# Head attention: two of the eight high parts of a head written by converting transfers on GpSimd's queue

## The chip, the cores and the metric

The kernel runs on one core of a Trainium2 chip. Its time is the device time of one execution in microseconds (us). Three runs of the kernel before gave 2814.51, 2816.11 and 2816.17 us; the median is 2816.11 us. The trace is that of a separate, profiled execution.

Engines are named as in the profile: PE is TensorE's matmul row and PEld its weight load, DVE is VectorE, ACT is ScalarE, POOL is GpSimd, SP is SyncE, which only issues transfers here.

## The reference

The program is a chain of six sublayers on `x` of shape (4, 1024, 128): a mixture-of-experts layer, an attention with shared query, key and value, the mixture-of-experts layer again, a recurrent layer, a second attention with gates and cumulative sums, and the recurrent layer again. The change touches the first attention alone:

```
b, t, c = x.shape            # 4, 1024, 128; x is the layer-normalised input
y = x.reshape(b, t, nh, hs).transpose(0, 2, 1, 3)        # 16 heads of 8 dimensions
scores = einsum('bhtk,bhsk->bhts', y, y) / sqrt(hs)
attn = softmax(scores)
o = einsum('bhts,bsc->bhtc', attn, x)                    # each head weights all 128 channels
return o.transpose(0, 2, 1, 3).reshape(b, t, nh * c) @ weight
```

There are 4 x 16 = 64 heads in all. For each the scores are 1024 x 1024; a head's output is 1024 x 128.

## The kernel before

Products are kept near float32 by splitting each factor into a high part (a `float32r` copy, rounded by the conversion) and a low part (the float32 value less the high part), and by summing three matmuls: low times high, high times low, high times high. These are lines 88, 89 and 90, in the helper `product`.

`head_attention` runs one block in which every engine has a program written out by hand in program order; semaphores alone tie them. A head is cut into 8 tiles `s` of 128 rows by 1024 columns (`TILES` = 8), and the running number of a tile is `n = 8 h + s`. For a tile

- PE writes the scores (line 797, four matmuls a tile pair stand on four row groups and run side by side), for two tiles at a time,
- ACT takes the exponential from PSUM into `heads_e`, which has four buffers `e[:, s % 4, :]` (line 849), and sums the rows on the way (its second instruction, the accumulator's read, after which `exp_done` is counted),
- the high part `heads_e_hi` is written by ACT for tiles 1, 3, 5, 7 (line 856) and by DVE for tiles 0, 2, 4, 6 (line 907),
- DVE writes the low part `heads_e_lo`, exponential less high part (line 909), tile by tile, and counts `low`,
- PE multiplies the parts with the value's parts into the head's output (`weighted_rows`, lines 88 to 90), six tiles behind the scores (`TRAIL` = 6), so that tiles 0 and 1 of a head follow the scores of tiles 6 and 7 of the same head, and tiles 2 to 7 follow scores of the next head.

Around that, per head: DVE inverts the sums (lines 865 and 868); SP stores them and loads them back spread over all partitions as `heads_scale` (512 KB, line 759); DVE multiplies the head's output by it, two halves, `heads_u` (line 875), ACT and DVE split that (lines 839 and 881), and PE adds the head's product with the output weights (`add_head`). DVE's program has `heads_u` of head h - 1 after tile 5 of head h, and the low parts of `heads_u` after tile 7. PE has `add_head` of head h - 2 after the scores of tiles 6 and 7 and directly ahead of tile 0's products of head h, and that tile's first matmul writes over the output, so it waits until `heads_u` has read it.

The scores' operands come from DRAM by eight transfers of 64 KB a head and side: `heads_right` on SP's queue, `heads_left` on POOL's queue (line 743). POOL does nothing else in this stage. It issues head h + 1's eight loads once head h - 1's last scores are done, a whole head ahead.

Of the kernel before, what the change touches and what calls it, by code (L numbers as in the profile page):

```python
# [73 lines left out]
def f(ap):  # L74

    return ap.bitcast(F32)
# [601 lines left out]
def head_attention(nc, tag, psum, consts, dram, x):  # L678


    with ExitStack() as ctx:
# [12 lines left out]
                  splits=[(dram["head_w"], w_hi[:, :], w_lo[:, :])], copies=[(parts_dram[:, 0, :], 0), (parts_dram[:, 1, :], 1), (parts_dram[:, 2, :], 0)],  # L694
                  copied=copied)

        left = sb(f"{tag}_left", [P, 2, T], F32R)
        right = sb(f"{tag}_right", [P, 2, T], F32R)
        v_hi, v_lo = sb(f"{tag}_v_hi", [P, TOKENS], F32R), sb(f"{tag}_v_lo", [P, TOKENS], F32R)
        e = sb(f"{tag}_e", [P, 4, T])  # L700
        sums = sb(f"{tag}_sums", [P, 2, TILES])
        inverse = sb(f"{tag}_inverse", [P, 2, 32])
        inverse_rows = sb(f"{tag}_inverse_rows", [P, 2, 32])
# [12 lines left out]
        out_done, scaled_ready, u_high, u_low = sem("out"), sem("scaled"), sem("u_high"), sem("u_low")  # L716
        sum_done, added = sem("sum_done"), sem("added")
        HEAD_LOADS = 8
        ACT_HIGH = (1, 3, 5, 7)
        TRAIL = 6  # L720
        COUNT = BATCH * HEADS
        VALUE_BANKS = TOKENS // BANK

        def highs(h, s):

            by_act = sum(i in ACT_HIGH for i in range(s + 1))
            return h * len(ACT_HIGH) + by_act, h * (TILES - len(ACT_HIGH)) + (s + 1 - by_act)

        def turned_value(k):

# [15 lines left out]
        with nc.Block() as block:  # L746
# [18 lines left out]
            @block.gpsimd  # L765
            def _(pool):
                load_head(pool, left, (0, 0), 0, left_loaded)
                load_head(pool, left, (0, 0), 1, left_loaded)
                for h in range(2, COUNT):
                    pool.wait_ge(scores_done, (h - 1) * TILES)  # L770
                    load_head(pool, left, (0, 0), h, left_loaded)

            @block.tensor
            def _(pe):
# [24 lines left out]
                        last.then_inc(scores_done, 1)  # L799

                def weighted_rows(h, s):
                    pe.wait_ge(low, h * TILES + s + 1)
                    at_v = slice(h // HEADS * T + s * P, h // HEADS * T + (s + 1) * P)
                    for half in range(HALVES):
                        at = slice(half * BANK, (half + 1) * BANK)
                        if s == 0:
                            after(pe, scaled_ready, (h - 1) * HALVES + half + 1)
                        last = product(pe, psum[:, OUT + half, :], (v_hi[:, at_v], v_lo[:, at_v]),
                                       (e_hi[:, s, at], e_lo[:, s, at]), first=s == 0, last=s == TILES - 1)
                    last.then_inc(out_done, 1)  # L810
# [22 lines left out]
            @block.scalar  # L833
            def _(act):
                def u_highs(g):
                    after(act, sum_done, g - 1)
                    for half in range(HALVES):
                        act.wait_ge(scaled_ready, g * HALVES + half + 1)
                        act.copy(u_hi[:, g % 2, half, :], u[:, half, :]).then_inc(u_high, 1)

                for k in range(0, 2 * VALUE_BANKS, 2):
                    act.wait_ge(turned, k + 1)
                    act.copy(turned_value(k), psum[:, k % 8, :]).then_inc(v_by_act, 1)
                for n in range(COUNT * TILES):
                    h, s = n // TILES, n % TILES
                    act.wait_ge(scores_done, n + 1)
                    after(act, low, n - 3)
                    wide = psum[:, SCORES + 2 * (s % 2):SCORES + 2 * (s % 2) + 2, :].rearrange("p a b -> p (a b)")
                    act.activation(e[:, s % 4, :], wide, ACT.Exp, scale=HEAD ** -0.5,  # L849
                                   accum_out=sums[:, h % 2, s:s + 1]).then_inc(exp_done, 1)  # L850
                    if s in ACT_HIGH:
                        act.wait_ge(exp_done, n + 1)
                        after(act, out_done, n - (TILES - 1))
                        if n < BATCH:
                            act.wait_ge(copied[n], BATCH_COPIED)
                        act.copy(e_hi[:, s, :], e[:, s % 4, :]).then_inc(act_high, 1)  # L856
                    if s == TILES - 1 and h >= 1:
                        u_highs(h - 1)
                u_highs(COUNT - 1)

            @block.vector
            def _(dve):
                def invert(g):
                    dve.wait_ge(exp_done, (g + 1) * TILES)
                    dve.reciprocal(inverse[:, g % 2, 0:TILES], sums[:, g % 2, :]).then_inc(divided, 1)
# [29 lines left out]
                for n in range(COUNT * TILES):  # L895
                    h, s = n // TILES, n % TILES
                    if s == 0 and h >= 1:
                        invert(h - 1)
                    high_act, high_dve = highs(h, s)
                    if s in ACT_HIGH:  # L900
                        dve.wait_ge(act_high, high_act)
                    else:
                        dve.wait_ge(exp_done, n + 1)
                        after(dve, out_done, n - (TILES - 1))
                        if n < BATCH:
                            dve.wait_ge(copied[n], BATCH_COPIED)
                        dve.tensor_copy(e_hi[:, s, :], e[:, s % 4, :]).then_inc(dve_high, 1)
                        dve.wait_ge(dve_high, high_dve)
                    dve.tensor_tensor(e_lo[:, s, :], e[:, s % 4, :], f(e_hi[:, s, :]), ALU.subtract).then_inc(low, 1)  # L909
                    if s == TRAIL - 1 and h >= 1:  # L910
                        scale_sums(h - 1)
                    if s == TILES - 1 and h >= 1:
# [837 lines left out]
```

## Time and profile before

| | us |
|---|---|
| median of three runs | 2816.11 |
| the profiled execution, its own time | 2814.1 |
| its span, first to last instruction | 2812.3 |
| of it, the head stage | 665 to 1672 |
| PE busy in the head stage | 980.26 of 1007 |
| DVE busy in the head stage | 960.00 of 1007 |
| ACT busy in the head stage | 881.45 of 1007 |

The profiled execution is 2.0 us below the median of the runs and 1.8 us longer than its span. In the head stage TensorE was granted 0.99 of its full clock. PE and DVE both look full there, so the shares don't tell which one holds the other; the order in time within one head does. Times in the tables below are microseconds from the span's start.

### The profile page before, as it was taken

To read this page: it belongs to the slowest core of one execution; us is meant where nothing else is said; L and a number is where in the kernel's file an instruction comes from. 1 tells how busy PE (TensorE), PEld (TensorE's weight loads), DVE (VectorE), ACT (ScalarE), POOL (GpSimd) and SP (SyncE) were. 2 spreads that over 40 slices of the span, in tenths; PEclk is the share of its full clock that TensorE was granted. 3 is DMA by queue.
4 is the path that set the end of the run, shared out by engine and by line. 5 is a ranking of instruction groups with operands and counts; after the bars stand their busy time and mean duration, and the time that the engine had idled before them with its cause. 6 is when DMAs were issued, how large, how long until landed. Compare 5 with 4: busy or idle time off the path is not lost. (4 is left out here: it accounts for less than half of the span.)

```text
span 2812.3 us, 36464 instructions
## 1 busy us (share of the span) xinstructions
PE 2633.2 (94%) x11619; PEld 1977.0 (70%) x11619; DVE 2253.9 (80%) x3349; ACT 1829.7 (65%) x3092; POOL 1232.4 (44%) x1265
## 2 busy tenths in 40 slices
PE   7899999997999999999999997999999989788788
PEld 4688888874666666666666664888888866577566
DVE  5777777777999999999999978777787765578545
ACT  3355555556888888888888863555555555466565
POOL 2466667664232323233333312666666650345200
PEclk9999999998999999999999999999999999789899
DMA  2566666644333333333333323466666610100000
GB/s 63 125 140 137 147 140 131 148 99 150 103 101 103 101 105 99 106 98 107 101 104 100 106 71 75 108 147 143 134 147 146 132 42 1 38 8 8 8 8 30
DMA packets 107391, 271.55 MB, mean 97 GB/s; under 512 B 30784, under 2 KB 35648, under 8 KB 107072
## 3 DMA queue, kind: packets, MB, share of 16 engines
q1 hardware_dynamic: 82192, 235.41, 33.8%
q0 software_dynamic: 24576, 33.62, 4.3%
q8 instruction: 92, 1.51, 0.2%
q14 instruction: 99, 0.81, 0.1%
q10 hardware_dynamic: 432, 0.20, 0.0%
HBM read 258.35 MB, written 10.76 MB: 96 GB/s over the span
## 5 line engine op out<-in xcount | busy, mean ns | idle before, releaser
L628 POOL TENSOR_TENSOR moe_experts_lo<-moe_experts_hidden,moe_experts_hi 128x512 fp32r<-128x512 f32 x512 | 660.9, 1291 | 342.2 <-ACT moe_experts_hi L566 342.1
L909 DVE TENSOR_TENSOR heads_e_lo<-heads_e,heads_e_hi 128x1024 fp32r<-128x1024 f32 x512 | 616.2, 1224 | 25.8
L573 ACT ACTIVATE psum<-psum 128x512 f32<-128x512 f32 x512 | 298.0, 582 | 479.4 <-PE psum L90 479.4
L743 POOL DMA_DIRECT2D heads_left<-heads_parts x512 | 306.7, 612 | 670.2 <-PE psum L797 610.6
L849 ACT ACTIVATE heads_e<-psum 128x1024 f32<-128x1024 f32 x512 | 520.0, 1023 | 107.2 <-PE psum L797 107.2
L600 DVE TENSOR_TENSOR moe_experts_weighted<-moe_spread,psum 128x512 f32<-128x512 f32 x512 | 351.1, 686 | 190.7 <-PE psum L90 186.8
L88 PE MATMUL psum<-heads_e_hi,heads_v_lo 128*128 128x512 f32 x1024 | 429.6, 419 | 18.1 <-DVE heads_u L875 18.1
L88 PE MATMUL psum<-moe_n_hi,moe_w_lo 128*128 128x512 f32 x1024 | 400.8, 391 | 6.0 <-PEq L54 6.0
L89 PE MATMUL psum<-heads_e_lo,heads_v_hi 128*128 128x512 f32 x1024 | 404.1, 395 | 0.0
L90 PE MATMUL psum<-heads_e_hi,heads_v_hi 128*128 128x512 f32 x1024 | 400.9, 392 | 0.0
L89 PE MATMUL psum<-moe_n_lo,moe_w_hi 128*128 128x512 f32 x1024 | 400.1, 391 | 0.0
L90 PE MATMUL psum<-moe_n_hi,moe_w_hi 128*128 128x512 f32 x1024 | 399.8, 390 | 0.0
L605 DVE TENSOR_TENSOR moe_experts_hidden<-moe_experts_weighted,psum 128x512 f32<-128x512 f32 x512 | 352.0, 687 | 34.9 <-POOL moe_experts_lo L628 17.9
L566 ACT CAST moe_experts_hi<-moe_experts_hidden 128x512 fp32r<-128x512 f32 x512 | 313.4, 612 | 1.3 <-DVE moe_experts_hidden L605 1.3
L88 PEld LDWEIGHTS psum<-heads_e_hi,heads_v_lo 128*128 128x128 f32 x1024 | 192.5, 188 | 124.6 <-issue 67.6
L856 ACT CAST heads_e_hi<-heads_e 128x1024 fp32r<-128x1024 f32 x256 | 269.6, 1053 | 8.1
L88 PEld LDWEIGHTS psum<-moe_n_hi,moe_w_lo 128*128 128x128 f32 x1024 | 193.3, 189 | 48.3 <-POOLq L638 7.4
L90 PEld LDWEIGHTS psum<-heads_e_hi,heads_v_hi 128*128 128x128 f32 x1024 | 193.1, 189 | 45.3
L90 PEld LDWEIGHTS psum<-moe_n_hi,moe_w_hi 128*128 128x128 f32 x1024 | 193.3, 189 | 40.3
L89 PEld LDWEIGHTS psum<-moe_n_lo,moe_w_hi 128*128 128x128 f32 x1024 | 193.4, 189 | 40.1
L89 PEld LDWEIGHTS psum<-heads_e_lo,heads_v_hi 128*128 128x128 f32 x1024 | 193.3, 189 | 32.6
L88 PE MATMUL psum<-moe_experts_hi,moe_w_lo 128*128 128x512 f32 x512 | 199.8, 390 | 2.4 <-POOL moe_experts_lo L628 2.4
(412 smaller groups left out, 4314.3 us busy)
## 6 DMA issues: line engine op xcount, KB each, us to landing
moe_spread<-moe_mask SPq DMA_DIRECT2D x128, 1024.0 KB, 10.4
heads_right<-heads_parts SPq DMA_DIRECT2D x512, 64.0 KB
heads_left<-heads_parts POOLq DMA_DIRECT2D x512, 64.0 KB, 2.5
heads_scale<-heads_inverse_copy SPq DMA_DIRECT2D x64, 512.0 KB, 3.7
moe_experts_raw<-in_gate SPq DMA_DIRECT2D x16, 256.0 KB, 11.7
moe_experts_raw<-in_up SPq DMA_DIRECT2D x16, 256.0 KB, 11.7
moe_experts_raw<-in_down SPq DMA_DIRECT2D x16, 256.0 KB, 11.7
heads_parts<-heads_e_hi SPq DMA_DIRECT2D x16, 256.0 KB, 2.4
```

Of the source, the lines that this page charges most:

```text
L88: pe.matmul(out, w_lo, x_hi, start=first, stop=False, skip_group_check=True)
L89: pe.matmul(out, w_hi, x_lo, start=False, stop=False, skip_group_check=True)
L90: return pe.matmul(out, w_hi, x_hi, start=False, stop=last, skip_group_check=True)
L566: act.copy(hi[:, p, :], hidden[:, p % 2, :]).then_inc(high_ready, 1)
L573: act.activation(psum[:, GATE + p % 2, :], psum[:, GATE + p % 2, :], ACT.Silu).then_inc(silu_ready, 1)
L600: dve.tensor_tensor(weighted[:, p % 2, :], spread[:, pair % 2, p, j * BANK:(j + 1) * BANK], psum[:, UP + p % 2, :], ALU.mult).then_inc(wei ...
L605: dve.tensor_tensor(hidden[:, p % 2, :], weighted[:, p % 2, :], psum[:, GATE + p % 2, :], ALU.mult).then_inc(hidden_ready, 1)
L628: pool.tensor_tensor(lo[:, p, :], hidden[:, p % 2, :], f(hi[:, p, :]), ALU.subtract).then_inc(low_ready, 1)
L743: eng.dma_start(f(tile[row:row + 2 * HEAD, h % 2, :]), parts_dram[dims, order:order + 2, at]).then_inc(loaded[h % 2], 16)
L849: act.activation(e[:, s % 4, :], wide, ACT.Exp, scale=HEAD ** -0.5, accum_out=sums[:, h % 2, s:s + 1]).then_inc(exp_done, 1)
L856: act.copy(e_hi[:, s, :], e[:, s % 4, :]).then_inc(act_high, 1)
L909: dve.tensor_tensor(e_lo[:, s, :], e[:, s % 4, :], f(e_hi[:, s, :]), ALU.subtract).then_inc(low, 1)
```

## The change

The high parts of tiles 2 and 5 are no longer written by DVE and ACT. POOL issues for each a transfer from `heads_e` (float32) to `heads_e_hi` (float32r), 128 partitions x 1024 elements, 512 KB, which converts on the way, and which has a semaphore of its own per tile. DVE keeps the high parts of tiles 0, 4 and 6, ACT those of tiles 1, 3 and 7. DVE writes the low parts in the order 0, 1, 3, 4, 2, 6, 7, 5. `heads_e` has five buffers in place of four, and `n % 5` picks the buffer. ACT's exponential of tile n waits for the low part of tile n - 5; PE's products of a tile wait until the low parts of this tile and of all tiles before it are written. POOL's loads of `heads_left` for head h + 1 now stand behind the transfer of tile 2 of head h and ahead of that of tile 5.

```diff
+        RING = 5
-        e = sb(f"{tag}_e", [P, 4, T])
+        e = sb(f"{tag}_e", [P, RING, T])
...
-        ACT_HIGH = (1, 3, 5, 7)
+        ACT_HIGH, DVE_HIGH, MOVED_HIGH = (1, 3, 7), (0, 4, 6), (2, 5)
+        LOW_ORDER = (0, 1, 3, 4, 2, 6, 7, 5)
+        LOWS_AFTER = {0: (0,), 1: (1,), 2: (), 3: (3,), 4: (4, 2), 5: (), 6: (6,), 7: (7, 5)}
+        moved = {s: sem(f"moved{s}") for s in MOVED_HIGH}
...
-                for h in range(2, COUNT):
-                    pool.wait_ge(scores_done, (h - 1) * TILES)
-                    load_head(pool, left, (0, 0), h, left_loaded)
+                for h in range(COUNT):
+                    for s in MOVED_HIGH:
+                        n = h * TILES + s
+                        pool.wait_ge(exp_done, n + 1)
+                        after(pool, out_done, n - (TILES - 1))
+                        if n < BATCH:
+                            pool.wait_ge(copied[n], BATCH_COPIED)
+                        pool.dma_start(e_hi[:, s, :], e[:, n % RING, :]).then_inc(moved[s], 16)
+                        if s == MOVED_HIGH[0] and 2 <= h + 1 < COUNT:
+                            pool.wait_ge(scores_done, h * TILES)
+                            load_head(pool, left, (0, 0), h + 1, left_loaded)
...
-                    pe.wait_ge(low, h * TILES + s + 1)
+                    pe.wait_ge(low, max(lows(h * TILES + i) for i in range(s + 1)))
...
-                    after(act, low, n - 3)
+                    if n >= RING:
+                        act.wait_ge(low, lows(n - RING))
...
+                def split(h, s):
+
+                    n = h * TILES + s
+                    high_act, high_dve = highs(h, s)
+                    if s in ACT_HIGH:
+                        dve.wait_ge(act_high, high_act)
+                    elif s in MOVED_HIGH:
+                        dve.wait_ge(moved[s], 16 * (h + 1))
+                    else:
...
+                        dve.tensor_copy(e_hi[:, s, :], e[:, n % RING, :]).then_inc(dve_high, 1)
+                        dve.wait_ge(dve_high, high_dve)
+                    dve.tensor_tensor(e_lo[:, s, :], e[:, n % RING, :], f(e_hi[:, s, :]), ALU.subtract).then_inc(low, 1)
...
-                    high_act, high_dve = highs(h, s)
-                    if s in ACT_HIGH:
-                        dve.wait_ge(act_high, high_act)
-                    else:
...
+                    for j in LOWS_AFTER[s]:
+                        split(h, j)
                     if s == TRAIL - 1 and h >= 1:
                         scale_sums(h - 1)
```

DVE's program from the inversion of one head's sums to the low parts of `heads_u` in the next; before, a high part (CAST) stands ahead of every second pair of low parts (`heads_e_lo`), and six low parts stand ahead of `heads_u`:

```order
L865 RECIPROCAL heads_inverse<-heads_sums 128x8
L868 STREAM_TRANSPOSE heads_inverse_rows<-heads_inverse 128x32
L907 CAST heads_e_hi<-heads_e 128x1024
L909 TENSOR_TENSOR heads_e_lo<-heads_e,heads_e_hi 128x1024 x2
L907 CAST heads_e_hi<-heads_e 128x1024
L909 TENSOR_TENSOR heads_e_lo<-heads_e,heads_e_hi 128x1024 x2
L907 CAST heads_e_hi<-heads_e 128x1024
L909 TENSOR_TENSOR heads_e_lo<-heads_e,heads_e_hi 128x1024 x2
L875 TENSOR_TENSOR heads_u<-heads_scale,psum 128x512 x2
L907 CAST heads_e_hi<-heads_e 128x1024
L909 TENSOR_TENSOR heads_e_lo<-heads_e,heads_e_hi 128x1024 x2
L881 TENSOR_TENSOR heads_u_lo<-heads_u,heads_u_hi 128x512 x2
```

The same stretch of DVE's program in the changed kernel; the first three low parts are those of tiles 0, 1, 3, the next two of tiles 4 and 2, the last three of tiles 6, 7, 5:

```order
L898 RECIPROCAL heads_inverse<-heads_sums 128x8
L901 STREAM_TRANSPOSE heads_inverse_rows<-heads_inverse 128x32
L892 CAST heads_e_hi<-heads_e 128x1024
L894 TENSOR_TENSOR heads_e_lo<-heads_e,heads_e_hi 128x1024 x3
L892 CAST heads_e_hi<-heads_e 128x1024
L894 TENSOR_TENSOR heads_e_lo<-heads_e,heads_e_hi 128x1024 x2
L908 TENSOR_TENSOR heads_u<-heads_scale,psum 128x512 x2
L892 CAST heads_e_hi<-heads_e 128x1024
L894 TENSOR_TENSOR heads_e_lo<-heads_e,heads_e_hi 128x1024 x3
L914 TENSOR_TENSOR heads_u_lo<-heads_u,heads_u_hi 128x512 x2
```

One CAST is gone, one low part has moved from ahead of `heads_u` to behind it, and between the CAST of tile 4 and `heads_u` there are two low parts in either kernel.

POOL's program of the stage before, all loads of the scores' left operand:

```order
L743 DMA heads_left<-heads_parts 16x1x1024 x512
```

POOL's program in the changed kernel, from its start to head 2's loads:

```order
L750 DMA heads_left<-heads_parts 16x1x1024 x16
L783 DMA heads_e_hi<-heads_e 128x1024 x3
L750 DMA heads_left<-heads_parts 16x1x1024 x8
L783 DMA heads_e_hi<-heads_e 128x1024 x2
L750 DMA heads_left<-heads_parts 16x1x1024 x8
```

Two converting transfers now stand between one head's eight loads and the next head's: tile 5 of a head, then tile 2 of the next.

## Rows read from the trace of the kernel before

**Rows 1.** The page's first line, and the head stage by windows (columns as named).
```profile
span 2812.3 us, 36464 instructions
...
core 0: us, PE busy (x) PEld busy (x) DVE busy (x) ACT busy (x) POOL busy (x), PEclk, DMA share, GB/s
665.00:1672.00 1007.00, 980.26 (x4509) 677.81 (x4508) 960.00 (x1161) 881.45 (x1413) 302.95 (x506) 0.99 0.33 101
```

**Rows 2.** Timeline of DVE over one head: start, us, engine, line, operation.
```profile
1055.01 1.28 DVE L875 TENSOR_TENSOR heads_u<-heads_scale,psum 128x512 f32<-128x512 f32 x2
1056.20 0.69 DVE L907 CAST heads_e_hi<-heads_e 128x1024 fp32r<-128x1024 f32 x1
1056.93 2.36 DVE L909 TENSOR_TENSOR heads_e_lo<-heads_e,heads_e_hi 128x1024 fp32r<-128x1024 f32 x2
...
1061.46 2.36 DVE L909 TENSOR_TENSOR heads_e_lo<-heads_e,heads_e_hi 128x1024 fp32r<-128x1024 f32 x2
...
1067.24 0.69 DVE L907 CAST heads_e_hi<-heads_e 128x1024 fp32r<-128x1024 f32 x1
1067.96 2.59 DVE L909 TENSOR_TENSOR heads_e_lo<-heads_e,heads_e_hi 128x1024 fp32r<-128x1024 f32 x2
1070.47 1.28 DVE L875 TENSOR_TENSOR heads_u<-heads_scale,psum 128x512 f32<-128x512 f32 x2
```

**Rows 3.** Timeline of PE in that head.
```profile
1058.74 0.50 PE L797 MATMUL psum<-heads_right,heads_left 32*128 32x512 f32 x4
...
1068.97 0.51 PE L797 MATMUL psum<-heads_right,heads_left 32*128 32x512 f32 x4
...
1070.45 0.39 PE L89 MATMUL psum<-heads_u_lo,heads_w_hi 128*128 128x512 f32 x1
1070.68 0.40 PE L90 MATMUL psum<-heads_u_hi,heads_w_hi 128*128 128x512 f32 x1
1071.30 0.47 PE L88 MATMUL psum<-heads_e_hi,heads_v_lo 128*128 128x512 f32 x1 [0.22 <-DVE heads_u L875]
```

**Rows 4.** Waits in the head stage: total us, times, longest.
```profile
PE psum L88 <- DVE heads_u L875: 18.1, 63, 1.8
```

**Rows 5.** Timeline of ACT in that head.
```profile
1063.62 0.20 ACT L849 ACTIVATION_READ_ACCUMULATOR heads_e<-psum 128x1 f32 x1
...
1064.86 1.05 ACT L856 CAST heads_e_hi<-heads_e 128x1024 fp32r<-128x1024 f32 x1
...
1067.01 0.19 ACT L849 ACTIVATION_READ_ACCUMULATOR heads_e<-psum 128x1 f32 x1
...
1068.24 1.06 ACT L856 CAST heads_e_hi<-heads_e 128x1024 fp32r<-128x1024 f32 x1
...
1070.52 1.02 ACT L849 ACTIVATE heads_e<-psum 128x1024 f32<-128x1024 f32 x1
```

**Rows 6.** Groups by line: count, busy us, mean ns, idle before.
```profile
L907 DVE CAST heads_e_hi<-heads_e 128x1024 fp32r<-128x1024 f32 x256 | 174.6, 682 | 11.9 <-ACT heads_e L849 5.1
...
L856 ACT CAST heads_e_hi<-heads_e 128x1024 fp32r<-128x1024 f32 x256 | 269.6, 1053 | 8.1
```

**Rows 7.** POOL: timeline of one head's loads, one of them alone, and the tile's summary.
```profile
1069.82 4.83 POOL L743 DMA_DIRECT2D heads_left<-heads_parts  x8 [10.63 <-PE psum L797]
...
1071.43 1.02 POOL L743 DMA_DIRECT2D heads_left<-heads_parts  x1
...
L743 POOL DMA_DIRECT2D heads_left<-heads_parts x512: 542/562/1027, 661.2 to 1632.5; - x171
DMA to landing us min/median/max: 2.2/2.5/5.0
```

**Rows 8.** Transfers: SP's issue of the scale; landings by line; SP's queue, 1063.9 to 1066.2.
```profile
1063.05 0.34 SPq L759 DMA_DIRECT2D heads_scale<-heads_inverse_copy  x1
...
heads_scale<-heads_inverse_copy SPq DMA_DIRECT2D x64, 512.0 KB, 3.7
heads_parts<-heads_e_hi SPq DMA_DIRECT2D x16, 256.0 KB, 2.4
...
q1 hardware_dynamic: 156, 0.57, 83.8%
```

More of the change, by code:

```diff
@@ L724, in highs, with lows @@
         def highs(h, s):
-            by_act = sum(i in ACT_HIGH for i in range(s + 1))
-            return h * len(ACT_HIGH) + by_act, h * (TILES - len(ACT_HIGH)) + (s + 1 - by_act)
+            return tuple(h * len(tiles) + sum(i <= s for i in tiles) for tiles in (ACT_HIGH, DVE_HIGH))
+        def lows(n):
+            return n // TILES * TILES + LOW_ORDER.index(n % TILES) + 1
         def turned_value(k):
@@ L846, in _ @@
                     act.wait_ge(scores_done, n + 1)
-                    after(act, low, n - 3)
+                    if n >= RING:
+                        act.wait_ge(low, lows(n - RING))
                     wide = psum[:, SCORES + 2 * (s % 2):SCORES + 2 * (s % 2) + 2, :].rearrange("p a b -> p (a b)")
-                    act.activation(e[:, s % 4, :], wide, ACT.Exp, scale=HEAD ** -0.5,
+                    act.activation(e[:, n % RING, :], wide, ACT.Exp, scale=HEAD ** -0.5,
                                    accum_out=sums[:, h % 2, s:s + 1]).then_inc(exp_done, 1)
@@ L855, in _ @@
                             act.wait_ge(copied[n], BATCH_COPIED)
-                        act.copy(e_hi[:, s, :], e[:, s % 4, :]).then_inc(act_high, 1)
+                        act.copy(e_hi[:, s, :], e[:, n % RING, :]).then_inc(act_high, 1)
                     if s == TILES - 1 and h >= 1:
@@ L862, in _ @@
             def _(dve):
+                def split(h, s):
[6 more added lines that the diff above has]
+                    else:
+                        dve.wait_ge(exp_done, n + 1)
+                        after(dve, out_done, n - (TILES - 1))
+                        if n < BATCH:
+                            dve.wait_ge(copied[n], BATCH_COPIED)
+                        dve.tensor_copy(e_hi[:, s, :], e[:, n % RING, :]).then_inc(dve_high, 1)
+                        dve.wait_ge(dve_high, high_dve)
+                    dve.tensor_tensor(e_lo[:, s, :], e[:, n % RING, :], f(e_hi[:, s, :]), ALU.subtract).then_inc(low, 1)
                 def invert(g):
@@ L898, in _ @@
                         invert(h - 1)
-                    high_act, high_dve = highs(h, s)
-                    if s in ACT_HIGH:
-                        dve.wait_ge(act_high, high_act)
-                    else:
[L903 to L909, printed above, removed]
+                    for j in LOWS_AFTER[s]:
+                        split(h, j)
                     if s == TRAIL - 1 and h >= 1:
```

## The prediction

> **What bounds the kernel now.** I read the windows first. In the head stage (1007 us, 36% of the span) PE is busy 980 and DVE 960 us, ACT 881 [rows 1]. Two engines that full say that the stage runs in step, not who sets the step. So I read one head in order of time, PE first, then what PE waits for, back to PE.
>
> A head lasts 15.46 us (`heads_u` starts at 1055.01 and again at 1070.47 [rows 2]), and 64 heads fill the stage. On PE the reader is to see one hole. The matmuls of `add_head` follow each other at 0.23 us (1070.45, 1070.68); the next one, the first of tile 0's products, could start at 1070.91 and starts at 1071.30, released by `heads_u` [rows 3]. The list of waits has this pair 63 times, once per head from the second [rows 4]. Its 18.1 us count only the time after the modelled end of a matmul; from start to start the hole is 0.39 us a head, 24.6 us in all. That is the most that relief of DVE can give here, however much work is taken off it.
>
> Why is `heads_u` late? Backwards: it starts at 1070.47, as the two low parts before it (tiles 4 and 5) end at 1067.96 + 2.59 = 1070.55. Elsewhere two low parts in a row take 2.36 us (at 1056.93, at 1061.46) [rows 2], so here 0.23 us is a wait: ACT's high part of tile 5 runs from 1068.24 to 1069.30 [rows 5], and tile 5's low part needs it. Ahead of them stands DVE's CAST of tile 4 at 1067.24 [rows 2], which starts 0.04 us after the exponential of tile 4 is done (1067.01 + 0.19 = 1067.20 [rows 5]); that exponential follows PE's scores at once. So the loop is PE's scores of tiles 4 and 5, exponential 4, CAST 4, two low parts, `heads_u`, PE. Only what lies on it counts.
>
> **The change part by part.**
>
> Removed from DVE: 64 CASTs of 682 ns, 44 us; from ACT: 64 of 1053 ns, 67 us [rows 6]. Neither shortens the loop by itself. The CAST that goes is tile 2's, ahead of the exponential of tile 4: DVE then waits longer for ACT's high part of tile 3, which ends at 1064.86 + 1.05 = 1065.91 as before [rows 5], and CAST 4 still starts at 1067.24. I cost these at nothing; PE's own pace covers them.
>
> On the loop, the second low part behind CAST 4 is now tile 2's in place of tile 5's. Tile 5's waited for ACT; tile 2's waits for its transfer. If that has landed, the pair takes 2.36 us in place of 2.59: `heads_u` starts at 1070.24 and PE's hole shrinks from 0.39 to 0.16 us. Gain: 0.23 us x 63 heads = 14.5 us.
>
> The transfer of tile 2 is the added wait. Behind it on DVE stands `heads_u`, for which PE waits, so lateness is paid one for one. Its time: exponential 2 is done at 1063.62 + 0.20 = 1063.82 [rows 5]. POOL starts an issue 0.34 us after its release (scores end at 1068.97 + 0.51 = 1069.48 [rows 3], issue at 1069.82 [rows 7]), so this one at 1064.16. The low part of tile 2 could start half a pair after 1067.96, at 1069.14. The transfer has 4.98 us from issue to landing for the whole gain, and 5.21 for no change.
>
> No row shows a converting transfer, nor one of 512 KB from POOL. The nearest rows: POOL's 64 KB land in 2.5 us (median) with an issue of 0.56 us [rows 7]. SP's queue used 83.8% of 16 engines for 2.3 us to move 0.57 MB [rows 8], which makes 1.77 us for 512 KB (0.524 MB) and 0.22 for 64 KB; so 2.5 + 1.55 = 4.05 us. From SP, 512 KB of the scale land in 3.7 us, and 256 KB out of `heads_e_hi`, from SBUF, in 2.4 us, which gives 3.3 for twice as much [rows 8]. The lower end is 2.5 us. The upper: issue time that grows with the rows, 8 x 0.56 in place of 0.56, makes 4.05 + 3.9 = 8.0 us. I take 4.05, the row of the same queue.
>
> Something else is then in the way. The inversion of the sums moves behind one more low part (tile 5's), 1.18 us, so SP issues the scale's 512 KB at 1063.05 + 1.18 = 1064.23 in place of 1063.05 [rows 8]: within 0.1 us of POOL's transfer. If the two share the engines packet by packet all the way, mine is later by the other's 1.77 us: 5.82 us. The Trainium skill (DMA: Bandwidth & Descriptors, "Queues, rings and completion order" and "Issuing engines are not separate DMA queues") says that transfers of all queues run on the same 16 engines, which take turns between queues packet by packet; by that rule the full 1.77 us would be paid. The same page ("Anatomy of one DMA") puts a transfer from GpSimd's queue at about 2.0 us and its bytes at 436 GB/s, an estimate of 3.2 us here alone, which no run shows yet; with the full collision it would still be in time. I take half of the collision, 0.9 us: the rows of SP's transfers (3.7 for 512 KB, next to eight loads issued right behind it) argue that 4.05 is rather too much. That makes 4.94 us against 4.98, in time with nothing to spare.
>
> The transfer of tile 5 stands behind eight loads of `heads_left` on POOL's queue: 1064.16 + 0.56 + 4.83 [rows 7] = 1069.55, landing at 1073.6. DVE reaches low part 5 after those of tiles 6 and 7, 1059.29 - 1055.01 = 4.28 us after `heads_u`, at 1074.52. Were it later, DVE has slack up to the wait for ACT's high part of tile 3 in the next head: from `heads_u` to the end of low part 1 it needs 1063.82 - 1055.01 + 1.18 = 9.99 us, to 1080.23, and that high part ends at 1065.91 + 15.23 = 1081.14. So 1.8 us in all cover it; beyond that it costs one for one.
>
> The loads themselves start 1.5 tiles into the head instead of a head ahead: the last is issued at 1068.99 and lands by 1071.5; PE's next scores need it at 1058.74 + 15.23 = 1073.97 [rows 3]. 2.5 us cover it. One of the eight takes 1.02 us because it lies beside a DVE CAST [rows 7]; the transfer of tile 2 lies between CASTs 0 and 4 and meets none.
>
> The scale lands at 1064.23 + 3.7, at worst + 1.77, 1069.7, before `heads_u` at 1070.24. The fifth buffer makes ACT's exponential of tile 7 wait for the low part of tile 2, which ends at 1070.32, 0.2 us before the 1070.52 at which it starts now [rows 5]. PE's wait for all earlier low parts falls on tiles 2 and 5, whose products come in the next head, over 3 us later. Nothing there.
>
> Sum, against the profiled execution's own 2814.1 us: 2814.1 - 14.5 = 2799.6; the median of the runs is 2.0 us above it, so 2801.6, say 2802 us.
>
> **The rivals.**
>
> *Collision in full.* The scale's and tile 2's transfers share the engines all the way: landing after 5.82 us, 0.61 past break-even, x 63 = 38 us more: 2854 us. For it: the two issues within 0.1 us. Against: the scale's own landing of 3.7 us. It decides from a landing of 5.21 us on, and this is the slower side. Between 5.1 and 5.3 us the time is within 0.2% of before.
>
> *Conversion or issue is slow.* 128 rows cost eight times the issue of 16, or converting packets run at a fraction of the rate: 8.0 us, and 2.8 us late x 63 = 176 us: 2992 us. Against: the packets are whole rows of 4 KB as in the other loads; the issue may cost the same for more rows.
>
> *POOL's queue is the new wait.* An issue of 2 us in place of 0.56 (tile 2's and tile 5's) makes tile 5's transfer land at 1073.6 + 2.9 = 1076.5, 1.1 past its cover of 1075.4: 69 us more, 2885 us; tile 2's would be late too.
>
> *Nothing changes.* Low part 2 lands a little late, or another wait on `heads_u` takes up the 0.23 us: 2811 to 2821 us.
>
> **How the numbers follow.** In time: 0.46, 2798 to 2810 us by itself (the 0.39 us hole whole would give 2791). Nothing changes: 0.14. Collision in full: 0.27, 2822 to 2862. POOL's queue: 0.06. Slow conversion: 0.07. A difference under 0.2%, 5.6 us, can't be told from none in a measurement of this kernel. So faster 0.46, same 0.14, slower 0.40. The range is 2797 to 2860 us: it holds in-time and unchanged cases and nearly all of the collision, and leaves out some 0.17.
>
> **What would show it.** Right: low parts 4 and 2 take 2.36 us back to back, the start of tile 0's products trails the last matmul of `add_head` by 0.39 us in place of 0.62, a head lasts 15.23 us. Converting transfers land under 5 us after issue, tile 5's before DVE asks, and `heads_left` before PE asks. Wrong: idle time on DVE ahead of the low part of tile 2 that ends with a DMA, scale landings near 5 us, POOL issues well over 1 us, or a head of 15.46 us with tile 2 in time.

## The result, and the profile after

The changed kernel took 3023.74 us (median of four runs, 3016.57 to 3031.97), the kernel before, on the same chip, 2815.31 us (2813.82 to 2816.17): ratio 1.0754, interval 1.0719 to 1.0788. It is 208 us slower, where 14 us faster was forecast.

The page's first line of the kernel after, and the head stage by windows, before and then after, each from the first scores to just behind the last, with the columns of [rows 1] (whose window reaches further and holds more matmuls):

```profile
span 3014.8 us, 36463 instructions
...
671.00:1659.00 988.00, 963.24 (x4415) 663.57 (x4416) 949.25 (x1145) 873.06 (x1400) 297.77 (x496) 0.99 0.33 101
...
668.00:1865.00 1197.00, 1022.67 (x4432) 704.81 (x4429) 906.40 (x1085) 814.91 (x1342) 347.24 (x624) 0.94 0.58 139
```

The span grew by 202.5 us, all of it in the head stage (from the first scores to the last it grew by 205). DVE and ACT do less work there, as meant, 906 and 815 us in place of 949 and 873. PE is busy some 56 us longer with no matmul added (from first to last scores, 4410 matmuls in either, 962.6 and 1018.4 us), its granted clock is 0.94 in place of 0.99, and the share of the DMA engines has gone from 0.33 to 0.58.

**Two holes a head on PE.** PE's timeline: first the last product ahead of a head's first scores in the kernel before (they start at 1058.74 [rows 3]); then, in the kernel after, the end of `add_head`, the next head's first scores, and two later heads' first scores with the products behind them:

```profile
1058.42 0.39 PE L90 MATMUL psum<-heads_e_hi,heads_v_hi 128*128 128x512 f32 x1
...
768.52 0.40 PE L90 MATMUL psum<-heads_u_hi,heads_w_hi 128*128 128x512 f32 x1
771.23 0.47 PE L88 MATMUL psum<-heads_e_hi,heads_v_lo 128*128 128x512 f32 x1 [2.31 <-DVE heads_u L908]
...
773.84 0.39 PE L90 MATMUL psum<-heads_e_hi,heads_v_hi 128*128 128x512 f32 x1
775.57 0.51 PE L812 MATMUL psum<-heads_right,heads_left 32*128 32x512 f32 x4 [1.34 <-issue]
...
851.84 0.50 PE L812 MATMUL psum<-heads_right,heads_left 32*128 32x512 f32 x4 [3.72 <-issue]
...
852.87 0.63 PE L89 MATMUL psum<-heads_e_lo,heads_v_hi 128*128 128x512 f32 x1
853.29 0.63 PE L90 MATMUL psum<-heads_e_hi,heads_v_hi 128*128 128x512 f32 x1
...
869.52 0.51 PE L812 MATMUL psum<-heads_right,heads_left 32*128 32x512 f32 x4 [0.61 <-DMA heads_left<-heads_parts]
...
870.29 0.40 PE L89 MATMUL psum<-heads_e_lo,heads_v_hi 128*128 128x512 f32 x1
870.53 0.40 PE L90 MATMUL psum<-heads_e_hi,heads_v_hi 128*128 128x512 f32 x1
```

The first is the hole of [rows 3]. It was to shrink from 0.62 to 0.39 us from start to start (1070.68 to 1071.30); here it is 2.71 us. The second was not there at all: before, the first scores of a head started 0.32 us after the last product in every head; here they wait, in some heads visibly for `heads_left`, in most for something that the profile doesn't name ("issue"). And behind a long hole the matmuls themselves are slow: from 852.87 on they follow each other at 0.42 us, where behind the short one (870.29, 870.53) it is 0.24. The windows of that stretch, in the hole, behind it and after it (the column before the last two is the granted clock):

```profile
848.50:851.80 3.30, 0.00 (x0) 0.00 (x0) 0.34 (x2) 0.00 (x0) 0.00 (x0) 1.00 0.39 122
851.80:855.30 3.50, 3.46 (x11) 2.67 (x12) 3.43 (x7) 2.89 (x5) 0.00 (x0) 0.57 0.00 0
855.30:862.00 6.70, 6.70 (x32) 4.60 (x32) 3.33 (x4) 4.67 (x9) 3.25 (x7) 0.97 0.66 189
```

PE stood idle for 3.3 us and was then granted 0.57 of its full clock on average (near the lower of its two levels, 1.2 and 2.4 GHz) for 3.5 us.

Starts alone give a sum without gaps. I cut each head on PE at four starts and add up over the 61 heads from the third to the last but one, after less before:

| part of a head on PE | before, us | after, us | more |
|---|---|---|---|
| last product to next head's first scores | 19.4 | 114.2 | 94.8 |
| first scores to the next scores (products of tiles 2 and 3 between them) | 208.6 | 246.9 | 38.3 |
| last matmul of `add_head` to tile 0's first product | 40.3 | 97.4 | 57.1 |
| tile 0's first product to tile 1's last | 158.2 | 169.8 | 11.6 |
| all else | 519.5 | 518.6 | -0.9 |
| sum | 945.9 | 1146.9 | 200.9 |

So 95 us are the wait ahead of a head's first scores and 57 us that for `heads_u`. The other 50 us, in the second and fourth row, are the clock behind these holes: PE never waits in these two parts in either kernel, and over them its granted clock averages 0.82 and 0.93, where it was 1.00 before.

**What came late.** Waits in the head stage of the kernel after (total us, times, longest), answering to [rows 4]:

```profile
DVE heads_e_lo L894 <- DMA heads_e_hi<-heads_e: 141.7, 93, 3.4
...
PE psum L812 <- issue: 78.5, 32, 4.2
PE psum L88 <- DVE heads_u L908: 76.1, 48, 3.3
...
PE psum L812 <- DMA heads_left<-heads_parts: 12.2, 14, 1.9
```

DVE over the same head, answering to [rows 2]; the low part at 769.26 is tile 2's, that at 776.00 tile 5's:

```profile
765.14 0.69 DVE L892 CAST heads_e_hi<-heads_e 128x1024 fp32r<-128x1024 f32 x1
765.86 1.23 DVE L894 TENSOR_TENSOR heads_e_lo<-heads_e,heads_e_hi 128x1024 fp32r<-128x1024 f32 x1
769.26 1.22 DVE L894 TENSOR_TENSOR heads_e_lo<-heads_e,heads_e_hi 128x1024 fp32r<-128x1024 f32 x1 [2.17 <-DMA heads_e_hi<-heads_e]
770.40 1.28 DVE L908 TENSOR_TENSOR heads_u<-heads_scale,psum 128x512 f32<-128x512 f32 x2
...
776.00 1.23 DVE L894 TENSOR_TENSOR heads_e_lo<-heads_e,heads_e_hi 128x1024 fp32r<-128x1024 f32 x1 [1.32 <-DMA heads_e_hi<-heads_e]
```

The transfers by line in the kernel after (KB each, median us from issue to landing), answering to [rows 8], and the two converting ones' issues on POOL, answering to [rows 7]:

```profile
heads_e_hi<-heads_e POOLq DMA_DIRECT2D x128, 512.0 KB, 6.8
heads_left<-heads_parts POOLq DMA_DIRECT2D x512, 64.0 KB, 5.3
heads_scale<-heads_inverse_copy SPq DMA_DIRECT2D x64, 512.0 KB, 4.4
...
L783 POOL DMA_DIRECT2D heads_e_hi<-heads_e x128: 527/558/645, 672.6 to 1859.8; - x128
```

The issue costs 0.56 us, as assumed. The landing doesn't hold: tile by tile the medians are 5.6 us for tile 2 (4.94 forecast) and 8.0 us for tile 5 (4.05 forecast), and `heads_left` went from 2.5 to 5.3 us. Who issued what, on POOL and SP, in the head above:

```profile
761.73 0.34 SPq L766 DMA_DIRECT2D heads_scale<-heads_inverse_copy  x1
762.02 0.55 POOL L783 DMA_DIRECT2D heads_e_hi<-heads_e  x1 [13.40 <-ACT heads_e L865]
762.11 5.71 SPq L750 DMA_DIRECT2D heads_right<-heads_parts  x8
762.55 4.45 POOL L750 DMA_DIRECT2D heads_left<-heads_parts  x8
766.97 0.59 POOL L783 DMA_DIRECT2D heads_e_hi<-heads_e  x1
```

Five times 512 KB are issued within some 6 us: the scale, tile 2, both sides of the scores' operands, tile 5. What the queues moved in 762.0 to 764.7, then in 764.7 to 766.2, then in 767 to 772, and last in 673.6 to 675.2 (head 0, where tile 2's transfer was alone); q0 is POOL's, q1 SP's, columns are packets, MB, share of the 16 engines:

```profile
q1 hardware_dynamic: 97, 0.40, 75.1%
...
q0 software_dynamic: 104, 0.41, 72.9%
q1 hardware_dynamic: 52, 0.15, 28.7%
...
q0 software_dynamic: 365, 0.62, 79.2%
q1 hardware_dynamic: 96, 0.26, 30.9%
...
q0 software_dynamic: 144, 0.52, 88.4%
```

In this head, up to 764.7, 2.7 us after tile 2's issue, only the scale's queue has moved anything. That goes with the two issues lying 0.3 us apart: in the 21 of the 61 heads in which they lie within 0.5 us of each other, tile 2 lands after 6.8 us (median), in the 11 in which the scale is issued over 0.5 us later, after 3.3 us. In the third stretch both queues together moved 0.88 MB in 5 us, 176 GB/s, with engines full; in the second, both were at work too and moved 0.55 MB in 1.5 us, 369 GB/s. Alone the converting transfer ran at 0.52 MB in 1.6 us, 328 GB/s.

The page has no landing for the right loads, but the trace has the increments of the semaphore that counts them, 72 a head. In 34 of the 47 heads whose scores wait over 0.3 us, the last increment comes 0.09 us ahead of the scores' start and after the last landing of `heads_left`; these heads make 84 of the 95 us, and the other 13, in which `heads_left` is the later, 11. From the last right load's issue to that increment the median is 7.3 us; before, it was 2.7 us, and the scores started 3.1 us after it.

### The profile page after: what moved, and what is told of

Same layout as the page of the kernel before. It is cut to its first block and busy times, and to the rows that moved or that the text cites. A ratio compares the mean times of both kernels' runs of the same rounds, so it can differ in the third digit from the quotient of the medians.

```text
span 3014.8 us, 36463 instructions
## 1 busy us (share of the span) xinstructions
PE 2689.6 (89%) x11619; PEld 2015.4 (67%) x11619; DVE 2207.3 (73%) x3285; ACT 1767.9 (59%) x3028; POOL 1283.4 (43%) x1393
## 5 line engine op out<-in xcount | busy, mean ns | idle before, releaser
L865 ACT ACTIVATE heads_e<-psum 128x1024 f32<-128x1024 f32 x512 | 521.1, 1024 | 374.3 <-PE psum L812 319.7
L88 PE MATMUL psum<-heads_e_hi,heads_v_lo 128*128 128x512 f32 x1024 | 450.3, 440 | 76.5 <-DVE heads_u L908 76.1
L783 POOL DMA_DIRECT2D heads_e_hi<-heads_e x128 | 73.0, 570 | 835.6 <-ACT heads_e L865 817.2
L89 PE MATMUL psum<-heads_e_lo,heads_v_hi 128*128 128x512 f32 x1024 | 422.8, 413 | 0.0
L90 PE MATMUL psum<-heads_e_hi,heads_v_hi 128*128 128x512 f32 x1024 | 420.8, 411 | 0.0
L88 PEld LDWEIGHTS psum<-heads_e_hi,heads_v_lo 128*128 128x128 f32 x1024 | 204.5, 200 | 188.1 <-DVE heads_e_lo L894 83.2
L750 POOL DMA_DIRECT2D heads_left<-heads_parts x512 | 285.9, 597 | 15.7 <-issue 10.3
L90 PEld LDWEIGHTS psum<-heads_e_hi,heads_v_hi 128*128 128x128 f32 x1024 | 205.5, 201 | 49.5
L89 PEld LDWEIGHTS psum<-heads_e_lo,heads_v_hi 128*128 128x128 f32 x1024 | 205.9, 201 | 36.7
L812 PE MATMUL psum<-heads_right,heads_left 32*128 32x512 f32 x1024 | 134.0, 510 | 99.0 <-issue 78.5
## 6 DMA issues: line engine op xcount, KB each, us to landing
moe_experts_raw<-in_gate SPq DMA_DIRECT2D x16, 256.0 KB, 11.6
```

The source lines that it names most:

```text
L88: pe.matmul(out, w_lo, x_hi, start=first, stop=False, skip_group_check=True)
L89: pe.matmul(out, w_hi, x_lo, start=False, stop=False, skip_group_check=True)
L90: return pe.matmul(out, w_hi, x_hi, start=False, stop=last, skip_group_check=True)
L750: eng.dma_start(f(tile[row:row + 2 * HEAD, h % 2, :]), parts_dram[dims, order:order + 2, at]).then_inc(loaded[h % 2], 16)
L812: last = pe.matmul(psum[:, SCORES + g, :], left[rows, h % 2, tile * P:(tile + 1) * P], right[rows, h % 2, half * BANK:(half + 1) * BANK], ...
L865: act.activation(e[:, n % RING, :], wide, ACT.Exp, scale=HEAD ** -0.5, accum_out=sums[:, h % 2, s:s + 1]).then_inc(exp_done, 1)
```

## The experiments

My theory was that the transfers take each other's time on the shared engines. The rivals: the conversion or POOL's issue is slow in itself, or the new order of the low parts or the fifth buffer is the cost.

**1. No conversion.** The converting transfers' destination is taken as float32, so the same bytes move as a plain copy; the rounding of these two tiles is left out.

```diff
-                        pool.dma_start(e_hi[:, s, :], e[:, n % RING, :]).then_inc(moved[s], 16)
+                        pool.dma_start(f(e_hi[:, s, :]), e[:, n % RING, :]).then_inc(moved[s], 16)
```

> The changed kernel, whose two transfers copy the bits without conversion (the rounding of the high parts of tiles 2 and 5 is left out), from the same queue at the same place. Theory 1: nothing changes, 3010 to 3035 us, landings 6 to 8 us. Theory 2: landings fall to about 4 us and the time to below 2860 us.

3022.57 us, 1.075 (1.0707 to 1.0793), like the changed kernel. Its transfers by line:

```profile
heads_e_hi<-heads_e POOLq DMA_DIRECT2D x128, 512.0 KB, 6.7
```

6.7 us against 6.8: conversion is free here, and that rival falls.

**2. The order alone.** No converting transfers: DVE casts tile 2 and ACT tile 5; the order of the low parts and five buffers stay.

```diff
-        ACT_HIGH, DVE_HIGH, MOVED_HIGH = (1, 3, 7), (0, 4, 6), (2, 5)
+        ACT_HIGH, DVE_HIGH, MOVED_HIGH = (1, 3, 5, 7), (0, 2, 4, 6), ()
```

> No converting transfers: the high part of tile 2 is DVE's again (in its turn, after low part 1), that of tile 5 ACT's; order of the low parts, five buffers and all waits as in the changed kernel; left loads a head ahead. This is a transfer that is always in time. The reading of the loop in the prediction (only the second low part ahead of heads_u counts): 0.23 us a head less, 2799 to 2806 us. Theory 3 (order and buffers cost the time): over 2830 us, up to 3024.

2806.34 us, 0.9982 (0.9963 to 1.0). DVE's timeline of one head:

```profile
1068.54 0.20 DVE L892 RECIPROCAL heads_inverse<-heads_sums 128x8 f32<-128x8 f32 x1
...
1074.23 0.69 DVE L878 CAST heads_e_hi<-heads_e 128x1024 fp32r<-128x1024 f32 x1
1074.95 2.36 DVE L888 TENSOR_TENSOR heads_e_lo<-heads_e,heads_e_hi 128x1024 fp32r<-128x1024 f32 x2
1077.23 1.28 DVE L902 TENSOR_TENSOR heads_u<-heads_scale,psum 128x512 f32<-128x512 f32 x2
...
1083.77 0.20 DVE L892 RECIPROCAL heads_inverse<-heads_sums 128x8 f32<-128x8 f32 x1
```

Low parts 4 and 2 take 2.36 us, and a head 15.23 us (1068.54 to 1083.77; the median of 61 heads too), the forecast's own two numbers, with every CAST still on its engine. Order and buffers are not the loss. The hole ahead of tile 0 shrinks by 13 us over the 61 heads, nearly the 14 that the transfers were to bring; 5 us come back ahead of the scores, and the time is only 5 us below that of the kernel before (2811.70), with an interval that touches 1. The run is a control as well: its scale and right loads start as late as in the changed kernel (scale 5.44 us after a head's first scores, 5.25 there), but the right loads land 3.7 us after the last one's issue, not 7.3, and the hole ahead of the scores grows by 5 us, not 95. Being issued later is not what makes them so late.

**3. Leaving transfers out of the changed kernel.** Each kernel leaves out loads from the third head on (the scale from head 2 on), so a later head works on an earlier one's operands. The edits delete these lines, or limit them to the first heads, and make the waits on them constant:

```diff
-                            load_head(pool, left, (0, 0), h + 1, left_loaded)
...
-                        load_head(sp, right, (0, 1), h + 2, right_loaded)
...
+                    if h < 2:
                        sp.dma_start(scale[:, h % 2, :], inverse_dram[h % 2:h % 2 + 1, :].to_broadcast([P, T])
```

Without the left loads:

> The changed kernel without the left loads of heads 2 to 63 (left out: each head from the third uses the left operand of head 0 or 1); nothing else stands on GpSimd's queue but the converting transfers. Theory 1 (crowding): if the left loads on the same queue are the cause, tile 5's transfer lands in about 4 us and the time falls to 2800 to 2830 us. If two queues at work at once are enough (right loads and scale on SP's queue beside it), landings stay at 5 to 6 us and the time near that of the run with the left loads ahead, 2900 to 2940 us.

Without the right loads:

> The changed kernel without the right loads of heads 2 to 63 (left out: operands of heads 0 and 1 are used again); left loads stand between the converting transfers as in the change, and the scale is loaded. If tile 5's transfer lands late (8.0 us) because it stands behind eight left loads on its own queue: still over 6 us, time over 2900 us. If it lands late because left and right loads run at once on two queues and slow each other: 3.5 to 5 us, left loads back at 2.5 to 3 us, and the time near that with neither (2847 us), 2840 to 2880 us.

Without the scale:

> The changed kernel without the scale's load from head 2 on (left out: the scales of heads 0 and 1 are used again); left and right loads as in the change. If the scale alone makes tile 2's transfer late: it lands in 3 to 3.5 us, and tile 5's still in 6 to 8 us, which then sets the head: 2900 to 2960 us. If left and right loads slow tile 2's as well: over 4.5 us and above 2960 us.

Without the loads of both sides:

> As the run before it, and without the right loads of heads 2 to 63 as well (left out: operands of heads 0 and 1 are used again). The scale's 512 KB per head is the only other transfer. Theory 1: tile 5's transfer lands 2.9 us after issue as in head 0, tile 2's in 2.9 us or, behind the scale, about 4.5 us: the stage is bound by PE again, 2798 to 2812 us in all. Otherwise, if the converting transfers are slow because engines work on the same memory, landings stay at 5 us and more, and the time above 2880 us.

Without all three:

> The changed kernel without left and right loads from head 2 on and without the scale's 512 KB load from head 2 on (all left out: operands and scales of heads 0 and 1 are used again). If the scale is what makes tile 2's transfer land after 5.7 us when there are no other loads: it lands in 2.9 us like tile 5's, the wait of PE on heads_u falls to what the order of low parts alone leaves, a head lasts 15.2 to 15.3 us, the whole 2795 to 2805 us. If a transfer issued at tile 2 is slow for another reason (engines at work on the same memory): it stays at 5 us and more, and the time at 2847 us.

The table has the median time and ratio, the median landings of tiles 2 and 5, and the two holes of the account above, over the same 61 heads, as us more than before:

| left out | us | ratio (interval) | tile 2, 5, us | ahead of scores | ahead of tile 0 |
|---|---|---|---|---|---|
| nothing | 3023.7 | 1.0754 (1.0719 to 1.0788) | 5.6, 8.0 | +95 | +57 |
| left | 2897.2 | 1.0295 (1.0268 to 1.0322) | 6.3, 6.0 | +21 | +56 |
| right | 2892.9 | 1.0319 (1.0249 to 1.0389) | 6.4, 4.9 | 0 | +75 |
| scale | 2917.6 | 1.0407 (1.0334 to 1.0481) | 3.3, 6.4 | +83 | -7 |
| left, right | 2847.3 | 1.0118 (1.0091 to 1.0144) | 5.7, 2.9 | 0 | +29 |
| all three | 2806.7 | 0.9972 (0.9955 to 0.9989) | 2.8, 2.9 | 0 | -12 |

The two holes have two causes. Take away the scale and tile 2 lands after 3.3 us, and its hole is gone, while the one ahead of the scores stays. Take away either side's loads and most or all of the hole ahead of the scores goes, while `heads_u` stays late. With all three gone a converting transfer lands in 2.8 to 2.9 us, so the engines' work on the same memory is not what made it slow, and `heads_u` and PE do what was forecast. Timelines of DVE and PE in the last kernel:

```profile
1322.85 2.36 DVE L889 TENSOR_TENSOR heads_e_lo<-heads_e,heads_e_hi 128x1024 fp32r<-128x1024 f32 x2
1325.13 1.28 DVE L903 TENSOR_TENSOR heads_u<-heads_scale,psum 128x512 f32<-128x512 f32 x2
...
1325.56 0.40 PE L90 MATMUL psum<-heads_u_hi,heads_w_hi 128*128 128x512 f32 x1
1325.95 0.47 PE L88 MATMUL psum<-heads_e_hi,heads_v_lo 128*128 128x512 f32 x1
```

0.39 us from start to start, -12 us over 61 heads where 0.23 x 61 = 14 was forecast. The wait ahead of the scores that the profile calls "issue" is thereby the right loads: it vanishes with them, and in the 32 heads of the changed kernel with that wait their last increment comes 0.09 us ahead of the scores, while `heads_left` had landed at least 0.9 us before. Two expectations missed. Without the loads of both sides I expected 2798 to 2812 us or over 2880; tile 2 lands after 5.7 us, where 2.9 or 4.5 was expected, and the time lies between. Without the right loads I expected 2840 to 2880 us, and tile 2 came later than in the changed kernel (6.4 us): in that run the scale is issued within 0.5 us of tile 2 in 51 of the 61 heads, in the changed kernel in 21, and in those heads tile 2 lands after 6.5 us, no later than there (6.8).

**4. Left loads moved.** In the changed kernel, issued at the head's start, ahead of tile 2's transfer:

```diff
+                    if 2 <= h + 1 < COUNT:
+                        pool.wait_ge(scores_done, h * TILES)
+                        load_head(pool, left, (0, 0), h + 1, left_loaded)
                     for s in MOVED_HIGH:
```

> The changed kernel, with GpSimd's loads of the scores' left operand issued a whole head ahead again, as before the change, and not between the converting transfers of tiles 2 and 5. Theory 1 (crowding: the eight left loads stand between the two converting transfers on one queue and drain beside the right loads and the scale): tile 5's transfer lands 4 to 5 us after issue in place of 8.4, no longer binds, left loads land in 2.5 us again; only tile 2's transfer still meets the scale, landing about 6 us after issue: 2800 to 2860 us. Theory 2 (a converting transfer is slow by itself while the engines work): landings stay at 6 to 8 us and the time above 2950 us. Theory 3 (the order of low parts and the fifth buffer cost the time): no change from 3024 us.

2928.0 us, 1.0424 (1.0381 to 1.0468); landings 5.3 and 6.3 us. Somewhat under half of the loss goes, less than I expected. The holes are +56 ahead of the scores and +31 us ahead of tile 0. The left loads are now in time (landed 12 us and more ahead of the scores), and in all 32 heads whose scores wait over 0.3 us the right loads' last increment comes 0.09 us ahead of them. It comes 5.9 us (median) after the last right load's issue; which of the transfers beside them holds the right loads up, no run separates.

The converse, in the kernel before: left loads issued only after the exponential of tile 2, beside the right loads, without any converting transfer.

```diff
-                    pool.wait_ge(scores_done, (h - 1) * TILES)
+                    pool.wait_ge(exp_done, (h - 1) * TILES + 3)
```

> The kernel before, with one edit: the left loads of the next head are issued after the exponential of tile 2, as the changed kernel does, in place of a head ahead. No converting transfer. Theory 1: the left loads meet the right loads and slow each other: left landing rises from 2.5 us towards 4 us, packets of 4 KB take 300 ns and more in place of 170, but the loads still land before the next head's scores, so the time stays at 2816 us within 6 us. Theories 2 and 3: landing stays at 2.5 us, time 2816 us.

2817.35 us, 1.0022 (1.0001 to 1.0044). Landings of `heads_left` in it:

```profile
DMA to landing us min/median/max: 2.3/4.1/6.5
```

Small loads on two queues side by side delay each other: the left ones land after 4.1 us in place of 2.5, the last right one after 5.6 us in place of 2.7. The cover just takes it; the hole ahead of the scores grows by 5 us. Only with the 1 MB of tiles 2 and 5 in the same stretch does it break.

**5. More room for the transfers.** The kernel of 4 with tile 5's low part behind the inversion of the sums, so that the inversion, the scale and the right loads behind it are not held up:

```diff
-        LOWS_AFTER = {0: (0,), 1: (1,), 2: (), 3: (3,), 4: (4, 2), 5: (), 6: (6,), 7: (7, 5)}
+        LOWS_AFTER = {0: (0,), 1: (1,), 2: (), 3: (3,), 4: (4, 2), 5: (), 6: (6,), 7: (7,)}
...
+                        split(h - 1, 5)
```

> Left loads a head ahead, and the low part of tile 5 moved behind the inversion of the sums, so that the scale is issued 1.2 us earlier, ahead of tile 2's transfer and not with it, and tile 5's transfer has some 1.7 us more. If the meeting of the scale with tile 2's transfer and the lateness of tile 5's are what is left of the loss: 2820 to 2870 us, the waits on transfers on DVE half of those with the left loads ahead alone (2928 us). If it is the rate at which two queues share the engines: 2890 to 2940 us.

2856.39 us, 1.0156 (1.013 to 1.0183). SP issues the scale 4.30 us after the head's first scores in place of 4.85 (medians), as in the kernel before (4.31), and the hole ahead of the scores falls from +56 to +17 us. Tile 2 still lands after 5.3 us, and DVE's waits on transfers fall from 46 to 29 us, not to the half that was expected.

Then also six buffers, `heads_u` one low part earlier (after tile 4's) and tile 2's low part behind it:

```diff
-        RING = 5
+        RING = 6
...
+        LOWS_AFTER = {0: (0,), 1: (1,), 2: (), 3: (3,), 4: (4,), 5: (2,), 6: (6,), 7: (7,)}
...
-                    if s == TRAIL - 1 and h >= 1:
+                    if s == TRAIL - 2 and h >= 1:
```

> The converting transfers kept, everything else moved out of their way: left loads a head ahead, low part 5 after the inversion, heads_u directly after tile 4's low part, tile 2's low part behind it (1.2 us later), six exponential buffers. If lateness of the transfers was all that cost the time, and tile 2's landing of 10.5 to 11 us after the head's first scores is now mostly in time (asked for at 11.6): 15.05 to 15.4 us a head, 2785 to 2810 us. If the transfers still come late in a third of the heads: 2815 to 2850 us. In neither case faster than the 2785 us of heads_u taken early without any transfer, whose head lasts 15.03 us with PE never waiting.

2853.8 us, 1.0146 (1.012 to 1.0172), far from the gain I expected. The hole ahead of tile 0 is gone (-24 us), that ahead of the scores is back at +56 us. Its waits:

```profile
PE psum L812 <- issue: 54.0, 32, 4.1
...
DVE heads_e_lo L894 <- DMA heads_e_hi<-heads_e: 2.9, 9, 0.6
```

Hardly anything waits for the converting transfers any more (2.9 us in all), and the kernel is still slower: they are paid by the loads that they hold up. These are the right loads: in all 32 heads whose scores wait over 0.3 us their last increment comes 0.09 us ahead of the scores, and the left ones had landed 12 us before. This kernel was not run without the converting transfers.

**6. `heads_u` earlier, nothing else.** The kernel before with `heads_u` after tile 4's low part:

```diff
-                    if s == TRAIL - 1 and h >= 1:
+                    if s == TRAIL - 2 and h >= 1:
```

> The kernel before, with heads_u of the head before taken one low part earlier (after tile 4's low part in place of tile 5's). No transfers, no fifth buffer. If the hole on PE is set by the chain exponential 4, CAST 4, low 4, low 5, heads_u, as the prediction read it, the hole of 0.39 us per head goes whole: 0.3 to 0.39 us x 63 heads, 2791 to 2798 us where before gives 2816. If DVE is the bound, not more than 0.1 us a head.

2785.49 us (2780.27 to 2787.84), 0.9901 (0.988 to 0.9922): 1% faster than the kernel before. PE's timeline in it:

```profile
1355.33 0.39 PE L90 MATMUL psum<-heads_u_hi,heads_w_hi 128*128 128x512 f32 x1
1355.56 0.40 PE L88 MATMUL psum<-heads_e_hi,heads_v_lo 128*128 128x512 f32 x1
```

The hole of 0.39 us in [rows 3] is gone entirely: 0.23 us from start to start. The prediction's bound for it was 24.6 us; 26 us came (over the 61 heads the hole had been 0.43 us on average).

## Why the prediction was wrong, point by point

- *The loop that sets a head's length*: right. PE's hole hung on `heads_u`, and that on what stands ahead of it on DVE: a head took 15.23 us (median) as soon as two low parts in a row met no wait (experiments 2 and 3), and experiment 6 emptied the hole.
- *The CASTs removed, POOL's issue, conversion*: right. 111 us of CASTs off DVE and ACT moved nothing by themselves (experiment 2, which keeps them, and the last kernel of 3, which lacks them, take 2806 and 2807 us), an issue of 128 rows took 0.56 us, conversion nothing.
- *The landing of tile 2 in 4.94 us*: wrong, and the first step that failed. "I take half of the collision" took 4.05 us for the transfer alone and 0.9 us for the scale. Alone it is 2.9 us, and beside the scale 5.7 us (no loads at all): the scale costs 2.8 us, more than its whole 1.77 us. The two errors went opposite ways, so it is luck that the rival *collision in full*, 5.82 us and 2854 us, comes near the kernel without the scores' loads, 5.7 us and 2847 us. In the changed kernel tile 2's lateness is the hole of 57 us ahead of tile 0, which goes with the scale's load. By the Trainium skill (DMA: Bandwidth & Descriptors, "Queues, rings and completion order") the engines take turns between queues packet by packet, a packet holding several descriptors; that was the case for the full price. The price came out above it: in the kernel without the scores' loads POOL's queue moves its first packet 3.3 us (median) after tile 2's issue, 1.1 us without the scale. The rows don't show where such a packet ends, so they don't decide whether the rule failed. The estimate from the same page of the Trainium skill ("Anatomy of one DMA"), 3.2 us for the transfer alone, was nearer to the 2.9 measured than my 4.05.
- *The loads "2.5 us cover it"*: wrong, and the larger failure. It let `heads_left` land in 2.5 us, its time in an empty stretch, though the change put it beside the right loads and between 1 MB of converting transfers: 5.3 us. The right loads were put at nothing without a reason, and they cost the most: from the last one's issue to its landing 7.3 us in place of 2.7, with 3.1 us of cover before. They stand behind the scale on SP's queue, which I had moved by 1.18 us (0.94 measured, from 4.31 to 5.25 us after a head's first scores, median) and followed no further; but the later issue alone costs 5 us (experiment 2), and what breaks the cover is what they meet. PE's first scores wait for both sides, 84 us for the right and 11 for the left, and most of the 50 us of clock follows. No rival had this wait, so none of them reached 3024 us; the range ended at 2860.
- *Tile 5 in time at 1073.6*: wrong in its landing (8.0 us), and DVE waits for it, 87 us in all ahead of its low part. What of it reaches PE isn't settled: the scale's issue, behind it on DVE, came no later (5.25 us) than from the move of the low part alone (5.44 us in experiment 2).
- *The clock*: no step of mine had it. It followed from the holes.
- *What would show it wrong*: the idle time ahead of tile 2's low part, ended by a DMA, was named and is there; the scale's landing went to 4.4 us, not 5.

## What to carry to other kernels

Before work is moved to DMA queues, add up all that is in flight in the stretch where the new transfers run, and price the landings of the others as well as the new ones': each of the transfers priced here looked covered by its own row, the right loads were not priced, and together they outran the covers. A queue that the change delays has to be followed to its last user, here from the scale to the loads behind it to the next head's scores. And where the stall is one of order, look for an order first: moving one step of DVE's program gave 1.0%, more than 111 us of relieved work was to bring.

## What the runs showed of the hardware

- Full engines don't always move the same: 176 GB/s in the stretch of both sides' loads and tile 5, 16 x 5 us x 1.10 / 0.88 MB = 100 engine-us per MB, against 54 for SP's queue alone in [rows 8] and 16 x 1.6 us x 0.884 / 0.52 MB = 44 for the converting transfer alone. Two busy queues are not enough for it: from 764.7 to 766.2 both moved 369 GB/s, 16 x 1.5 us x 1.016 / 0.55 MB = 44. Nor are they needed: from 762.0 to 764.7 the scale's queue, alone in the records, took 16 x 2.7 us x 0.751 / 0.40 MB = 81. What on the engines takes the time stays open.
- A converting transfer of 512 KB within SBUF, alone, lands in 2.9 us (head 0), quicker than 3.7 us for the scale from DRAM [rows 8].
- A hole of 3.3 us on PE was followed by 3.5 us at a granted clock of 0.57; one of 0.6 us (869.52) by none.
